# A four-layer gated model on one core: later layers placed anew in each body, score factors in two buffers, one product for the mixture's weights, the last heads' attention in two banks

## The reference, cut to what matters

```python
# x, ctx: (64, 64, 256); four layers in a row, each added to x through a tanh gate
x = x + tanh(g_xattn[0]) * attention(layernorm(x), ctx)   # 16 heads of 128, keys and queries normalised
x = x + tanh(g_ffn[0]) * mixture(layernorm(x))            # x@W.T + b, and 2 of 8 LoRA experts of rank 16
x = x + tanh(g_xattn[1]) * sigmoid_attention(layernorm(x), ctx, ctx)
x = x + tanh(g_ffn[1]) * experts(layernorm(x))            # 1 of 8 experts of rank 64

def mixture(x):                                           # x_flat: 4096 x 256
    base = x_flat @ W.T + b
    logits = x_flat @ gate_w.T + gate_b
    topk_logits, topk_idx = jax.lax.top_k(logits, 2)
    gates = softmax(topk_logits)
    xA = einsum('nd,erd->ner', x_flat, lora_A)
    delta = einsum('ner,eor->neo', xA, lora_B)            # the two chosen ones are kept
    return base + sum(delta_topk * gates)
```

## Time and profile before

| | |
|---|---|
| Time, median of 3 runs (lowest, highest) | 1403.92 us (1403.7, 1408.33) |
| The profiled execution: its time, its span | 1404.73 us, 1403.0 us |
| Granted TensorE clock, mean | 0.993 |
| PE busy, PEld busy | 1349.8 us (96%), 1185.6 us (85%) |
| DVE busy, ACT busy, POOL busy | 760.0 us (54%), 753.8 us (54%), 73.9 us (5%) |
| DMA, mean | 77 GB/s |

### The profile page before, as it was taken

The page is one execution under the profiler, slowest core; times in us unless marked ns, Lnnn a source line. Parts: engine busy times, 40 slices in busy tenths (PEclk is TensorE's granted clock), DMA queues, the critical chain, the costliest instruction groups (busy, mean ns, idle before and its releaser), DMA issues.

```text
span 1403.0 us, 27092 instructions
## 1 busy us (share of the span) xinstructions
PE 1349.8 (96%) x10647; PEld 1185.6 (85%) x10647; DVE 760.0 (54%) x2310; ACT 753.8 (54%) x2065; POOL 73.9 (5%) x114
## 2 busy tenths in 40 slices
PE   7799999999999999999999999999999999999888
PEld 7688888888898888888898878988889888888777
DVE  7544565446555465554654555544655545554475
ACT  3266666466464654646555564646646455556421
POOL 3000000010000100010000100001000010001010
PEclk9899999999999999999999999999999999999999
DMA  8211522132021221223112131123211212121100
GB/s 296 87 76 76 136 92 75 61 102 94 32 76 61 91 91 54 68 77 114 60 38 87 65 111 56 49 73 106 91 46 61 76 61 83 53 76 61 46 0 31
DMA packets 51452, 108.49 MB, mean 77 GB/s; under 512 B 8224, under 2 KB 32000, under 8 KB 50688
## 3 DMA queue, kind: packets, MB, share of 16 engines
q1 hardware_dynamic: 51328, 106.77, 22.9%
HBM read 89.98 MB, written 16.78 MB: 76 GB/s over the span
## 4 chain that ended last, share of the span: by engine, by line
PE 84%; DVE 11%; ACT 4%; issue 1%; DMA 0%; SPq 0%; DVEq 0%
PE bank L113 56%; PE bank L1033 7%; PE bank L1043 5%; PE bank L1008 3%; PE bank L1022 2%; PE bank L1145 2%; PE bank L1157 2%; DVE least L1504 1%; DVE logit L1502 1%; ACT xn L778 1%; PE bank L998 1%; PE bank L1182 1%; PE bank L1096 1%; DVE pt L1488 1%; DVE ao_lo L1493 1%
## 5 line engine op out<-in xcount | busy, mean ns | idle before, releaser
L1493 DVE SCALAR_TENSOR_TENSOR ao_lo<-bank,vecs,ao_hi 128x512 fp32r<-128x512 f32 x128 | 96.1, 750 | 192.0 <-ACT ao_hi L747 191.0
L113 PE MATMUL bank<-sv,ct_hi 128*128 128x256 f32 x1024 | 196.4, 290 | 0.0
L113 PE MATMUL bank<-so,ao_hi 128*128 128x256 f32 x1024 | 192.2, 286 | 1.7 <-DVE ao_lo L1493 1.7
L747 ACT ACTIVATE ao_hi<-bank,vecs 128x512 fp32r<-128x512 f32 x128 | 87.8, 686 | 175.8 <-PE bank L1033 175.7
L753 ACT ACTIVATE expo<-logit,least 128x64 f32<-128x64 f32 x512 | 171.4, 338 | 18.8 <-DVE least L1504 18.8
L113 PEld LDWEIGHTS bank<-so,ao_hi 128*128 128x128 f32 x1024 | 163.0, 189 | 12.6 <-issue 5.2
L113 PEld LDWEIGHTS bank<-sv,ct_hi 128*128 128x128 f32 x1024 | 156.4, 189 | 0.5 <-issue 0.5
L772 ACT ACTIVATE q_sb<-bank,qbias,qscale 128x512 f32<-128x512 f32 x128 | 99.5, 778 | 96.3 <-PE bank L113 95.9
L113 PE MATMUL bank<-so,ao_lo 128*128 128x256 f32 x512 | 143.4, 280 | 0.0
L113 PE MATMUL bank<-sv,ct_lo 128*128 128x256 f32 x512 | 142.9, 279 | 0.0
L1502 DVE TENSOR_TENSOR logit<-bank,rr 128x256 f32<-128x256 f32 x128 | 54.3, 424 | 157.4 <-PE bank L1043 157.2
(11 more groups left out here) (238 smaller groups left out, 2779.0 us busy)
## 6 DMA issues: line engine op xcount, KB each, us to landing
sv<-v_scratch SPq DMA_DIRECT2D x56, 512.0 KB, 3.4
so<-o_scratch SPq DMA_DIRECT2D x56, 512.0 KB, 3.2
xin<-in_x_dram SPq DMA_DIRECT2D x8, 512.0 KB, 5.4
cin<-in_ctx_dram SPq DMA_DIRECT2D x32, 128.0 KB, 4.9
xres<-in_x_dram SPq DMA_DIRECT2D x8, 512.0 KB, 4.4
c_scratch<-cs SPq DMA_DIRECT2D x8, 512.0 KB, 5.0
v_scratch<-sv SPq DMA_DIRECT2D x8, 512.0 KB, 2.9
o_scratch<-so SPq DMA_DIRECT2D x8, 512.0 KB, 2.6
```

Source lines behind the costliest of these rows:

```text
L113: last = pe.matmul(out, lhs[a], rhs[b], start=start and n == 0, stop=stop and n == 2, **kw)
L747: act.activation(ao_hi[:, :], pv_ps[:, :], ACT.Identity, bias=vecs[:, 4 * H + h % H:4 * H + h % H + 1]).then_inc(ao_hi_ready.sem, 1)
L1493: dve.scalar_tensor_tensor(out=ao_lo[:, :], in0=pv_ps[:, :], scalar=vecs[:, v:v + 1], in1=ao_hi[:, :].bitcast(F32), op0=ALU.add, op1=ALU.s ...
```

## The change

- **One product.** w0t and a0t become one tile m0t of M0 = 392 columns. For groups 0 to 6, `mixture_rows` multiplies each tile of tokens by all 392 columns, one tile to a bank, at (6,e), (7,b), (7,c), (7,d). ACT copies the first 136 columns out, and a new `mixture_base` on the DVE adds the other 256, times the gate, to xres. The bank of `mixture_lora` then holds the LoRA part alone. Group 7 (`LAST`) keeps two products.
- **New places.** The later layers' points are the same in all bodies. The two lora products move to (9,b), (9,c), gram products to (9,d), (9,e), (10,b), (10,d), x2's layer norm to (9,d), (9,e), (10,b), the second attention one step earlier, x3's layer norm to (13,e), (14,a), (14,b), xn3 to (14,d) of the body before, and the gate's transposes and products to steps 0 and 1.
- **Score factors.** rr has two buffers. `norms` moves from (15,e) to (14,b), `score_factors` for the next group from step 0 to (14,c). `split(b, 1)` now stands ahead of `attn_lo` in step 0.
- **The last heads.** Head 14 of group 7 uses bank 2 (`pj_ps[0]`) and a part of the key weights' tiles for its attention. The order of what remains of heads 12 to 15 is written out, and the gate products of group 6 come before it. In `end()`, ACT copies the mixture's rows, and group 7's gate products alternate with its expert products.

```diff
-    MIXTURE = [..., *(("xa", j, "S", lg0_ready) for j in range(2))]
+    MIXTURE = [..., *(("xa", t, "S", base_ready) for t in range(NT))]
...
-            ("gr", 0, "N", gr_read), ("gr", 1, "N", gr_read), ("lora", 0, "S", x2_ready),
-            ("gr", 2, "N", gr_read), ("gr", 3, "N", gr_read), ("lora", 1, "S", x2_ready),
-            *(("gr", n, "N", gr_read) for n in range(4, 2 * NT)), *CONTEXT,
-            *(("late", u, "W", late_lo) for u in range(7)), ("rk", 0, "N", rr_ready)]
+            *(("lora", j, "S", x2_ready) for j in range(2)), *(("gr", n, "N", gr_read) for n in range(2 * NT)),
+            *CONTEXT, ("rk", 0, "N", rr_ready), *(("late", u, "W", late_lo) for u in range(7))]
...
-    TURN_AT = {(7, "d"): 0, (7, "e"): 1, (8, "b"): 2, (8, "c"): 3}
-    GRAM_AT = {(9, "b"): 0, (9, "d"): 1, (10, "b"): 2, (10, "d"): 3}
-    CHOICE_AT = {"xn3": (0, "a"), ("xt3", 0): (1, "b"), ("xt3", 1): (1, "c"), ("lg", 0): (1, "e"), ("lg", 1): (2, "b"),
+    ROWS_AT = {(6, "e"): 0, (7, "b"): 1, (7, "c"): 2, (7, "d"): 3}
+    TURN_AT = {(7, "e"): 0, (8, "b"): 1, (8, "c"): 2, (8, "d"): 3}
+    GRAM_AT = {(9, "d"): 0, (9, "e"): 1, (10, "b"): 2, (10, "d"): 3}
+    CHOICE_AT = {"xn3": (14, "d"), ("xt3", 0): (H, "b"), ("xt3", 1): (H, "d"), ("lg", 0): (H + 1, "b"),
...
         def prob_transpose(g, h):
             pe.wait_ge(p_ready.sem, p_ready.count(g, h))
-            ao_ready.wait(pe, g, h - 1)
+            if (g, h) == (LAST, H - 2):
+                pj_read.wait(pe, g, 3 * H - 2)
+            else:
+                ao_ready.wait(pe, g, h - 2 if (g, h) == (LAST, H - 1) else h - 1)
...
+        def mixture_rows(s, t):
+            dst, cols, n = take("xa", t, s), slice(t * P, (t + 1) * P), C0 + E0 if s == LAST else M0
+            pe.wait_ge(xt1_ready.sem, xt1_ready.count(s, t // 2))
+            for c in range(DC):
+                last = three(pe, dst[:, 0:n], [v[:, c, cols] for v in x2t], [v[:, c, 0:n] for v in m0t],
+                             start=c == 0, stop=c == DC - 1)
...
+        def mixture_base(s, t):
+            if t == 0:
+                dve.wait_ge(x1b_ready.sem, x1b_ready.count(s, 0))
+            dve.wait_ge(xa_ready.sem, xa_ready.count(s, t))
+            dve.scalar_tensor_tensor(out=xres[:, t, :], in0=bank_of("xa", t, s)[:, C0 + E0:M0], scalar=tg[:, 2:3],
+                                     in1=xres[:, t, :], op0=ALU.mult, op1=ALU.add).then_inc(base_ready.sem, 1)
...
+        scores(LAST, H - 1)
+        output(LAST, H - 4)
+        attend(LAST, H - 3)
+        prob_transpose(LAST, H - 2)
+        attend(LAST, H - 2)
+        prob_transpose(LAST, H - 1)
+        output(LAST, H - 3)
+        attend(LAST, H - 1)
+        output(LAST, H - 2)
+        output(LAST, H - 1)
         end()
```

More of the change, by code:

```diff
@@ L904, in end @@
             for t in range(NT):
+                mixture_rows(LAST, t)
+            for t in range(NT):
                 expert_high(NEXT, t)
@@ L942, in _ @@
             step(LAST, h)
-        for h in range(ATT_LAG):
-            step(NG, h)
+        exps(LAST, H - 1)
+        attn_hi(LAST, H - 3)
+        prob_copy(LAST, H - 2)
+        expert_exp(NEXT)
+        attn_hi(LAST, H - 2)
+        prob_copy(LAST, H - 1)
+        attn_hi(LAST, H - 1)
         end()
@@ L1057, in output @@
                 s = slice(t * P, (t + 1) * P)
-                last = three(pe, o_ps[t // 2][:, (t % 2) * D:(t % 2 + 1) * D], (ao_hi[:, s], ao_lo[:, s]),
+                last = three(pe, o_ps[t // 2][:, (t % 2) * D:(t % 2 + 1) * D], (hi[:, s], lo[:, s]),
                              (so[:, p % 2, 0, h % 2, :], so[:, p % 2, 1, h % 2, :]),
@@ L1298, in awake @@
             for _ in range(n):
-                pe.matmul(bank[:, :], w0t[0][:, 0, 0:P], w0t[0][:, :, :].rearrange("p c d -> p (c d)"),
-                          start=True, stop=True)
+                pe.matmul(bank[:, :], a1t[0][:, 0, 0:P], a1t[0][:, 0, :], start=True, stop=True)
         def end():
@@ L1311, in end @@
             awake(take("xa", 0, LAST), 4)
-            for j in range(2):
-                mixture_rows(LAST, j)
+            for t in range(NT):
+                mixture_rows(LAST, t)
             for t in range(NT):
@@ L1345, in end @@
                 gate_logits(LAST, j)
-            for t in range(NT):
-                expert_rows(LAST, t)
+                expert_rows(LAST, j)
+            expert_rows(LAST, 2)
             expert_turned(LAST, 0)
+            expert_rows(LAST, 3)
             expert_turned(LAST, 1)
@@ L1384, in _ @@
             step(LAST, h)
-        for h in range(OUT_LAG):
-            step(NG, h)
+        scores(LAST, H - 1)
[8 more added lines that the diff above has]
+        output(LAST, H - 1)
         end()
@@ L1753, in step @@
                 probabilities(b, h - TURN_LAG)
+            if h == 0 and not is_body(b, 0) and live(b, 0):
+                split(b, 1)
             share(b, h, "a")
@@ L1763, in step @@
             share(b, h, "b")
-            if h == 0 and not is_body(b, 0) and live(b, 0):
-                split(b, 1)
-                score_factors(b)
             share(b, h, "c")
@@ L1788, in end @@
             context_sum(LAST)
-            for j in range(2):
-                mixture_logits(LAST, j)
             mixture_choice(LAST)
@@ L1865, in _ @@
                 step(b, h)
-        for h in range(ATT_LAG):
-            step(NG, h)
+        probabilities(LAST, H - 2)
+        logits(LAST, H - 1)
+        for j in range(2):
+            expert_logits(NEXT, j)
+        expert_choice(NEXT)
+        prob_copy(LAST, H - 2)
+        attn_lo(LAST, H - 3)
+        probabilities(LAST, H - 1)
+        attn_lo(LAST, H - 2)
+        prob_copy(LAST, H - 1)
+        expert_scale(NEXT)
+        attn_lo(LAST, H - 1)
         end()
```

265 lines of the change are left out of this document (120 added, 145 removed), and 6 rows, old and new, of tables (AT, LAST_AT).

## The result

The changed kernel takes 1387.12 us (median of 4 runs, 1385.94 to 1390.71), against 1403.81 us before in the same session: ratio 0.988, 95% interval 0.986 to 0.990. It is faster by 16.7 us, or 1.2%, with an interval that lies clear of 1. The time is inside the prediction's full range (1372 to 1389 us), but 1.1 us above the main case's own range (1375 to 1386 us), and 6.6 us above the predicted 1380.5 us. The profiled execution took 1385.94 us, with a span of 1384.2 us where the kernel before had 1403.0: 18.8 us less, where the sum said 23.7.

A forecast was written before the change was run, and what follows sets the result against it. PE, busy 96% of the span, was taken as the bound, so only its issue and waits count. Terms summed to -23.7 us: 1381.0 us from the profiled 1404.73, forecast 1380.5 us as median, full range 1372 to 1389.

The forecast's parts named there:

- main case: The sum of all terms holds: 1380.5 us, chance 0.55, own range 1375 to 1386 us.
- one product: Mixture rows, groups 0 to 6: one 392-column matmul replaces 136 and 256 columns, saving 0.052 us each, -8.7 us.
- start of a body: Step 0: PE's waits for xt_lo and ao_lo go, -10.1 us; late ao_lo and fuller step 14 cost +1.9 us.
- step 9: Six bodies: PE's 1.6 us wait for sums before the first lora product goes, -10.8 us.
- step 10: Six bodies: ten DVE scale links ahead of the sums lengthen PE's wait before the gram product, +11.7 us.
- last heads: End of group 7's attention: two banks, product order and normalisation behind the copy remove most idle time, -7.6 us.
- group 7's experts: Alternating 8-column with 512-column products keeps the clock up, and the wait for q_lo goes, -2.9 us.
- mixture's logits at the end: Group 7: the mixture's logits wait for an ACT copy, +0.4 us.
- body 0: First body: rr ahead of late weights' low parts costs +1.6 us, one step 9 wait less -0.4, together +1.2 us.
- clock in the bodies: Half-clock stretches follow the 2.3 us waits in two of six bodies, +1.2 us.
- a fall in most bodies: Sign of being wrong: the granted clock shows a fall in most bodies.

The follow-up runs named there:

- the scales moved alone: The changed kernel with only the DVE's scales of the second normalisation moved behind the sums of the third gram tile in step 10: span 1373.4 us.
- four refinements: Kernel with both moves, plus earlier gram sums, earlier tile scales, later first-body score factors, and last heads' probability copies ahead of attention copies: 1363.46 us.
- two products: The changed kernel with the 392-column product taken apart again into 136 and 256 columns: 1394.84 us.
- old order: Kernel with both moves, with step 9's lora products, their banks and x2's layer norm put back as before the change: span 1380.5 us.
- both moves: The changed kernel with the DVE's scales behind the sums and ACT's second normalisation behind the copy of values in step 10: 1368.04 us.
- normalisation moved alone: The changed kernel with only ACT's second normalisation moved one place later in step 10, behind the copy of values: span 1381.1 us.
- the two experiments: Both moves in step 10 of the changed kernel (1368.04 us), and step 9's order put back in the kernel with both moves (span 1380.5 us).
- the second profile: The changed kernel profiled once more with nothing edited: span 1388.4 us.
- The run with one bank: Kernel with both moves, with head 14's attention back in the bank of the others and the outputs a step earlier between them: span 1370.5 us.
- the old order back: Kernel with both moves, with group 7's gate products all ahead of the four expert products again: span 1369.5 us.

## Why the prediction was near, and what it missed

The sum of single waits carried most terms. The rival, that a removed wait turns up at the next user, describes the scales moved alone, a part of the start of a body, and two of the four refinements.

| term | predicted, us | measured, us | from |
|---|---|---|---|
| one product | -8.7 | -7.9 | 1.1 a body, two products |
| start of a body | -10.1 + 1.9 | -9.8 | what is left of body 3, below |
| step 9 | -10.8 | -10.8 | 1.8 a body, old order |
| step 10, six bodies | +11.7 | +12.0 | 2.0 a body, both moves |
| last heads | -7.6 | -6.0 | 26.17 against 32.15 |
| group 7's experts | -2.9 | -2.2 | 16.55 against 18.77 |
| mixture's logits at the end | +0.4 | +0.2 | waits for xg, 1.1 against 0.9 |
| body 0 | +1.2 | +0.6 | 138.6 against 138.0 |
| clock in the bodies | +1.2 | +3.3 | three falls of 1.6 against one of 1.5 |
| last body, step 10 | none | +2.1 | normalisation moved alone |

The right column sums to -18.5 us; the span moved by 18.8. For the middle bodies this is no independent check, since the start of a body is what the other terms leave of body 3. The start of a body is worked out: body 3 went from 165.30 to 162.94 us, -2.36, of which -1.12 is the product, -1.80 step 9 and +2.01 step 10, so that -1.45 is left for the start, in six bodies. To it comes body 1, where only xt_lo waited and whose step 0 went from 8.7 to 7.6 us.

- **Right, in mechanism and size:** the product, step 9, and step 10. The last is the wait that the change adds. It could be read from a trace that does not show it, because the wait there already existed (0.29 us), so that whatever goes ahead of it counts in full. The prediction's words "this term takes back all of step 9" are what the two experiments show.
- **A step that is missing:** in step 10 the prediction followed only the DVE. The same edit moves ACT's normalisation in the last body from behind the copy of values to ahead of it. In the middle bodies it is hidden behind the wait for the sums, but the last body has no gram product whose wait hides it, and there it costs 2.1 us. In the sum it takes the place of the 1.86 us wait for v_sb, which the prediction counted as gained.
- **A size:** the clock. Two falls in six were assumed at 1.2 us each; three came, at 1.6 us, and four in the second profile. That is 2 us in the sum, and up to 4 in a run. Four of six is a fall in most bodies, which the prediction had named as a sign of being wrong; the profile it was compared with had three.
- **Luck in a term:** body 0. The +0.6 us compares bodies with different falls of the clock: 138.02 us at 0.96 of full clock before, 138.61 us at 0.98 in the changed kernel. The run with one bank, whose edits lie behind body 0, had 0.96 again. Body 0 of the kernel before, and of that run:

```profile
48.26:186.28 138.02, 131.85 (x1016) 114.77 (x1017) 71.98 (x208) 82.39 (x234) 2.87 (x4) 0.96 0.31 101
```

```profile
48.25:188.55 140.30, 132.31 (x1017) 114.93 (x1017) 74.20 (x217) 83.06 (x236) 2.87 (x4) 0.96 0.31 99
```

  At like clock the term is +2.3 us, nearly twice the +1.2 us of the sum. A wait of 1.6 us for rr, as computed, is the larger part of it; the rest stays open.
- **The last heads:** two banks were credited with nearly all the idle time; 1.5 us of PE's remained, in three short waits, and these could not be removed by swapping two copies. Of the 6.0 us, bank and order are worth about 3 us by the run with one bank; the rest goes with the wait of 1.86 us for v_sb, which is gone, and with the clock, 0.95 before and 1.00 now.
- **Group 7's experts:** the cause was wrong. I put 1.7 us on 24 small products that bring the clock down. With the old order back the clock stayed up, and the order itself is worth 0.7 us. Why it fell there in the kernel before stays open.
- **The start of a body:** it gave 1.6 us more than the sum had, which offsets a part of what the other terms lack, and its split was wrong. The two waits share their cover with each other (1.4 and 1.2 us alone, 2.2 us together) and, as argued above, with the products for the norms, so that neither row gives the price of its own edit.

## What to carry to other kernels

When a chain of small dependent instructions moves on a helper engine, look for the first instruction behind it whose consumer already waits a little: there the whole chain is paid at once, while one place later it may cost nothing. Here the two moves behind it were worth 19 us (1387.12 to 1368.04), with the falls of the clock and the last body's wait that hang on it: more than the whole change had won. Follow every engine that the edit moves, in the first and last rounds too, since these lack the neighbour that hides it. And compare two profiles by equal stretches before crediting a difference of spans: twice here a span came out as forecast for a reason that the stretches refute.

## What the hardware showed

In the bodies 1 to 6 of the profiles here it came with 13 of 24 waits of 2.25 us (four profiles of three kernels) and with 3 of 12 waits of 1.6 us (two kernels). In the bodies 1 to 7 of four kernels it came with none of 32 waits of 0.7 to 1.5 us, and in the last body of five profiles with 2 of 5 waits of 1.9 us for v_sb. The place changes from one execution to the next. The Trainium skill (TensorE: Matmul & The Clock Gate, HAM oscillation) describes a wait for a transfer, longer than these, that brings the slow clock back every round; these traces agree only in part, with about one in two at 2.25 us. On average a wait of 2.25 us costs 13/24 x 1.6 = 0.9 us beyond its idle time, an estimate from these counts. In body 0 a fall or two more or less come and go in the same way, whichever kernel runs.

A fall needs no such wait. In the kernel before, the one among group 7's experts came behind 24 products of 8 columns with no idle time between them:

```profile
1383.11 0.25 PE L113 MATMUL bank<-g1t_hi,x2t_lo 128*128 128x8 f32 x1
1383.22 0.48 PE L113 MATMUL bank<-a1t_hi,x2t_hi 128*128 128x512 f32 x1
...
1384.54 0.63 PE L113 MATMUL bank<-a1t_lo,x2t_hi 128*128 128x512 f32 x1
1384.96 0.63 PE L113 MATMUL bank<-a1t_hi,x2t_lo 128*128 128x512 f32 x1
```

Here starts of products of 512 columns lie 0.42 us apart, at 1.2 GHz, where they lie 0.23 us apart otherwise. The same row of 24 products, in the run with the old order back, kept the clock at 1.00. The products of 8 columns start 0.11 us apart, as those of 136 columns do.
